# The causal mask added by DVE while it takes the maxima, and the window layers' turned keys of a batch in one row of columns

## The reference

```python
scores = jnp.einsum('bqhd,bkhd->bhqk', Q, K) / math.sqrt(D_K)
scores = jnp.where(causal, scores, -jnp.inf)
attn = jax.nn.softmax(scores, axis=-1)          # first attention
...
q = l2norm(q) * qs
k = l2norm(k) * ksc
q, k = rotary_xpos(q, k)
sim = jnp.einsum('bhwid,bhwjd->bhwij', bq, bk)  # bk: the window before, then its own
mask = (i < j) | (i > j + WINDOW) | (j == -1)
attn = jax.nn.softmax(jnp.where(mask, -big, sim), axis=-1)
```

## Time and profile before

| what | value |
|---|---|
| median of 3 runs | 1494.41 us (1487.76 to 1495.81) |
| the profiled execution | 1497.84 us |
| its span, first to last instruction | 1496.1 us |
| mean granted TensorE clock in it | 0.927 |
| busy: PE / DVE / ACT / POOL | 87% / 79% / 62% / 50% |

### The profile page before, as it was taken

How to read it: one execution, slowest core, us unless ns; L and a number is a source line. 1 busy time by engine, 2 the same in 40 slices (tenths; PEclk the granted TensorE clock), 3 DMA queues, 4 the chain that set the end, 5 groups by cost and what they waited for, 6 DMA issues and landing times. The chain is left out here.

```text
span 1496.1 us, 30910 instructions
## 1 busy us (share of the span) xinstructions
PE 1294.6 (87%) x11013; PEld 757.0 (51%) x11013; DVE 1180.9 (79%) x2532; ACT 934.8 (62%) x2597; POOL 742.3 (50%) x742
## 2 busy tenths in 40 slices
PE   5479999999999997459999999699689999997892
PEld 3234444444444443326666666565356666665551
DVE  6577888888888860659999999666599999996667
ACT  4416776777677765647888888332378888884230
POOL 2001212211221221469999999310499999993102
PEclk9859999999999997579999999889799999999896
DMA  4412121112111101100211111000002111110001
GB/s 115 132 61 68 35 60 44 37 36 60 43 37 39 33 4 50 50 21 23 51 35 31 30 30 30 8 1 1 21 23 49 30 30 30 34 32 9 1 1 56
DMA packets 35056, 55.40 MB, mean 37 GB/s; under 512 B 7106, under 2 KB 22732, under 8 KB 32588
## 3 DMA queue, kind: packets, MB, share of 16 engines
q1 hardware_dynamic: 34328, 53.27, 13.4%
q10 hardware_dynamic: 576, 0.15, 0.0%
HBM read 26.67 MB, written 8.39 MB: 23 GB/s over the span
## 5 line engine op out<-in xcount | busy, mean ns | idle before, releaser
L595 DVE TENSOR_REDUCE a_nm<-a_psM 128x1 f32<-128x512 f32 (+3 forms) x768 | 372.7, 550 | 101.8 <-PE a_psM L429 54.4
L516 ACT ACTIVATE a_prob<-a_psE 128x512 f32<-128x512 f32 (+3 forms) x768 | 319.4, 499 | 147.9 <-PE a_psE L444 146.1
L429 PE MATMUL a_psM<-a_ks,a_qs 72*128 72x512 bf16 (+3 forms) x768 | 253.0, 343 | 18.7 <-PEq L76 18.1
L444 PE MATMUL a_psE<-a_qs,a_ks 84*128 84x512 bf16 (+3 forms) x768 | 251.9, 336 | 13.2 <-ACT a_prob L516 6.9
L1080 POOL TENSOR_TENSOR w_t<-w_raw,w_sin 128x256 f32<-128x256 f32 x256 | 239.9, 966 | 47.2 <-ACT w_raw L1006 47.2
L551 POOL TENSOR_SCALAR_AFFINE_SELECT a_prob<-a_prob 128x512 f32<-128x512 f32 x128 | 81.1, 635 | 344.4 <-ACT a_prob L516 318.7
L1029 ACT ACTIVATE w_prob<-w_psS,w_bias 128x128 f32<-128x128 f32 x512 | 181.4, 367 | 49.9 <-DVE w_bias L1158 44.4
L1090 POOL TENSOR_TENSOR w_rn<-w_ssm,mhalf 128x16 f32<-128x16 f32 x64 | 189.4, 2960 | 3.1 <-DVE w_ssm L1128 3.1
L1085 POOL TENSOR_TENSOR w_rot<-w_t 128x1024 f32<-128x1024 f32 x64 | 152.0, 2374 | 8.8 <-issue 0.4
L458 PE MATMUL a_psO<-a_prob,v_all 128*32 128x512 f32 (+3 forms) x1536 | 148.1, 502 | 0.0
L444 PEld LDWEIGHTS a_psE<-a_qs,a_ks 84*128 84x128 bf16 x768 | 74.9, 98 | 142.7 <-issue 49.3
(11 more groups left out here) (139 smaller groups left out, 2508.3 us busy)
## 6 DMA issues: line engine op xcount, KB each, us to landing
w_vb<-w_v SPq DMA_DIRECT2D x128, 128.0 KB, 2.3
a_qs<-q_parts SPq DMA_DIRECT2D x16, 576.0 KB
a_ks<-k_parts SPq DMA_DIRECT2D x16, 576.0 KB
q_parts<-p_parts SPq DMA_DIRECT2D x24, 128.0 KB
k_parts<-p_parts SPq DMA_DIRECT2D x24, 128.0 KB
out_x<-l_y SPq DMA_DIRECT2D x8, 256.0 KB, 2.3
a_qs<-a_nmT SPq DMA_DIRECT2D x32, 48.0 KB
w_wqkv<-in_wqkv SPq DMA_DIRECT2D x2, 768.0 KB, 7.4
```

Source lines behind the costliest of these rows:

```text
L429: mm = pe.matmul(out, qs[0:ROWS, g, j, i * P:(i + 1) * P], ks[0:ROWS, g, j, 512 * kc:512 * kc + n], start=True, stop=not diag)
L444: pe.matmul(psE[:, r % NRING, 0:w], ks[0:KROWS, g, j, kt * P:(kt + 1) * P], qs[0:KROWS, g, j, q0:q0 + w], start=True, stop=True).then_inc( ...
L516: act.activation(prob[G % NPROB][:, j, 0:w], psE[:, r % NRING, 0:w], ACT.Exp, scale=SCALE0).then_inc(e_read, 1)
L595: dve.tensor_reduce(nm[:, s % 2, kc, i, j:j + 1], psM[:, r % MRING, 0:n], AX.X, ALU.max, negate=True).then_inc(m_read, 1)
```

## The change

In attend the mask matmul L432 goes. For the units that hold the diagonal DVE runs `tensor_tensor_reduce`: scores plus a mask of 512 columns (zeros, then the triangle), times -1, written back over the scores in PSUM, with a running minimum into the place of the negated maximum. Other units keep their reduction. In window the turned keys of the tiles of a batch lie side by side in one row of columns (two such rows, for batches in turn), so the 64 keys before a tile are already there: the copy L1151 and its semaphore go, and the score matmuls read 128 adjacent columns. The values' halves and the mask follow the new order of the keys.

```diff
--- before.py
+++ after.py
@@ -424,13 +424,9 @@
                     pe.wait_ge(stack_in[g], 32 * (s // NG + 1))
                 n = min(512, (i + 1) * P - 512 * kc)
                 out = psM[:, r % MRING, 0:n]
-                diag = kc == i // 4
                 ge(pe, m_read, r - MRING + 1)
-                mm = pe.matmul(out, qs[0:ROWS, g, j, i * P:(i + 1) * P], ks[0:ROWS, g, j, 512 * kc:512 * kc + n],
-                               start=True, stop=not diag)
-                if diag:
-                    mm = pe.matmul(out[:, n - P:n], sb["ident_b"], sb["mask_q"], start=False, stop=True)
-                mm.then_inc(m_ready, 1)
+                pe.matmul(out, qs[0:ROWS, g, j, i * P:(i + 1) * P], ks[0:ROWS, g, j, 512 * kc:512 * kc + n],
+                          start=True, stop=True).then_inc(m_ready, 1)
 
             def score(G, j):
 
@@ -585,6 +581,8 @@
         @block.vector
         def _(dve):
 
+            dve.wait_ge(sb["const_in"], 64)
+
             def maximum(u):
                 s, (i, j, kc) = u // NMU, MAX_UNITS[u % NMU]
                 r = max_slot(u)
@@ -592,7 +590,11 @@
                 if s > 1 and u % NMU in (0, NM_A):
                     dve.wait_ge(nm_parts, 2 * (s - 2) + (u % NMU == NM_A) + 1)
                 dve.wait_ge(m_ready, r + 1)
-                dve.tensor_reduce(nm[:, s % 2, kc, i, j:j + 1], psM[:, r % MRING, 0:n], AX.X, ALU.max, negate=True).then_inc(m_read, 1)
+                scores, low = psM[:, r % MRING, 0:n], nm[:, s % 2, kc, i, j:j + 1]
+                if kc == i // 4:
+                    dve.tensor_tensor_reduce(scores, scores, sb["mask_q"][:, 512 - n:512], -1.0, -3.0 * NEG, ALU.add, ALU.min, low).then_inc(m_read, 1)
+                else:
+                    dve.tensor_reduce(low, scores, AX.X, ALU.max, negate=True).then_inc(m_read, 1)
 
             def merge(s):
                 dve.wait_ge(m_read, max_slot(s * NMU + NMU - 1) + 1)
@@ -825,7 +827,7 @@
         raw = tile("w_raw", [P, 2, 2 * INNER])
         t1, t2 = tile("w_t1", [P, 2 * INNER]), tile("w_t2", [P, 2 * INNER])
         rot = tile("w_rot", [P, 2, 2 * INNER])
-        qT, kT = tile("w_qT", [P, 2, 4, P]), tile("w_kT", [P, 2, 4, KEYS])
+        qT, kT = tile("w_qT", [P, 2, 4, P]), tile("w_kT", [P, 2, 4, WIN + S])
         v = [tile(f"w_v{r}_", [P, INNER]) for r in range(4)]
         vb = [tile(f"w_vb{r}_", [P, INNER]) for r in range(4)]
         bias = tile("w_bias", [P, 2, HEADS])
...
@@ -868,8 +870,8 @@
 
                 at_least(sp, v_copied, base, t, 1)
                 halves(sp, av_done, t, -4)
-                sp.dma_start(vb[r][0:WIN, :], v[r][0:WIN, :]).then_inc(vb_in[r], 16)
-                sp.dma_start(vb[(r + 1) % 4][WIN:P, :], v[r][WIN:P, :]).then_inc(vb_in[r], 16)
+                sp.dma_start(vb[r][WIN:P, :], v[r][0:WIN, :]).then_inc(vb_in[r], 16)
+                sp.dma_start(vb[(r + 1) % 4][0:WIN, :], v[r][WIN:P, :]).then_inc(vb_in[r], 16)
 
             sp.wait_ge(zeroed, layer * 4 + 4)
             for t in range(NT):
@@ -908,21 +910,18 @@
                 p = r % 2
                 at_least(pe, qT_copied, base, t, 1)
                 at_least(pe, kT_copied, base, t, 1)
-                at_least(pe, prev_copied, base, t, 1)
                 halves(pe, exp_done, t, 0)
                 for w in range(2):
                     pe.matmul(psS[:, w, :].rearrange("p (c k) -> p c k", c=4), sb["ident_b"],
                               sb["mask_w"][:, t % TB, :].unsqueeze(1).broadcast_to((P, 4, P)), start=True, stop=False, skip_group_check=True)
+                half, first = t // TB % 2, t % TB * P
                 for c in range(4):
                     cols = slice(c * P, (c + 1) * P)
-                    for w in range(2):
-                        rows = slice(DH * w, DH * w + DH)
-                        lower = kT[rows, p, c, :].rearrange("p (a k) -> p a k", a=3)[:, 0:3:2, :]
-                        pe.matmul(psS[0:WIN, w, cols].rearrange("p (a k) -> p a k", a=2), qT[rows, p, c, 0:WIN], lower,
-                                  start=False, stop=True, skip_group_check=True)
-                    for w in range(2):
-                        rows = slice(DH * w, DH * w + DH)
-                        i = pe.matmul(psS[WIN:P, w, cols], qT[rows, p, c, WIN:P], kT[rows, p, c, 0:P], start=False, stop=True, skip_group_check=True)
+                    for u in range(2):
+                        for w in range(2):
+                            rows = slice(DH * w, DH * w + DH)
+                            i = pe.matmul(psS[WIN * u:WIN * u + WIN, w, cols], qT[rows, p, c, WIN * u:WIN * u + WIN],
+                                          kT[rows, half, c, first + WIN * u:first + WIN * u + P], start=False, stop=True, skip_group_check=True)
                 i.then_inc(s_done, 2)
 
             def turn_p(t, r, b):
@@ -1096,8 +1095,8 @@
         def _(dve):
 
             dve.memset(hT[WIN:P, 1, P:P + 1], 0.0).then_inc(zeroed, 1)
-            dve.memset(kT[:, 1, :, :], 0.0).then_inc(zeroed, 1)
-            dve.memset(vb[0][WIN:P, :], 0.0).then_inc(zeroed, 1)
+            dve.memset(kT[:, :, :, 0:WIN], 0.0).then_inc(zeroed, 1)
+            dve.memset(vb[0][0:WIN, :], 0.0).then_inc(zeroed, 1)
             dve.memset(ss[:, :, :, 1], 1e-24).then_inc(zeroed, 1)
 
             dve.wait_ge(w_in, WINDOW_LOADS)
@@ -1142,13 +1141,9 @@
                 dve.tensor_tensor(both, both, rn[:, p, :].unsqueeze(2).broadcast_to((P, 16, DH)), ALU.mult).then_inc(unit_done, 1)
 
             def copy_kT(t, r):
-                p = r % 2
                 at_least(dve, qkT_done, base, t, 1)
-                at_least(dve, prev_copied, base, t, 0)
-                dve.tensor_copy(kT[:, p, :, 0:P], psT[:, 1, :].rearrange("p (c n) -> p c n", c=4)).then_inc(kT_copied, 1)
-
-                halves(dve, s_done, t, -2)
-                dve.tensor_copy(kT[:, p, :, P:KEYS], kT[:, 1 - p, :, WIN:P]).then_inc(prev_copied, 1)
+                dve.tensor_copy(kT[:, t // TB % 2, :, WIN + t % TB * P:WIN + t % TB * P + P],
+                                psT[:, 1, :].rearrange("p (c n) -> p c n", c=4)).then_inc(kT_copied, 1)
 
             def maxima(t, r, w):
                 p = r % 2
@@ -1451,7 +1446,7 @@
             def early(name, shape, dt=F32):
                 return first.enter_context(nc.sbuf_tensor(name, shape, dt))[:]
 
-            sb["mask_q"] = early("mask_q", [P, P], BF16)
+            sb["mask_q"] = early("mask_q", [P, 512], BF16)
             sb["mask_k"] = early("mask_k", [P, P], BF16)
             sb["w_down"] = early("w_down", [P, 2 * DC])
             sb["w_uq"] = early("w_uq", [DC, D])
@@ -1496,7 +1491,7 @@
     bf, f = mybir.dt.np(BF16), np.float32
     c = {"c_ident": np.eye(P, dtype=f), "c_ident_b": np.eye(P).astype(bf)}
     i, j = np.arange(P)[:, None], np.arange(P)[None, :]
-    c["c_mask_q"] = np.where(j > i, NEG, 0.0).astype(bf)
+    c["c_mask_q"] = np.concatenate([np.zeros((P, 512 - P)), np.where(j > i, NEG, 0.0)], axis=1).astype(bf)
     c["c_mask_k"] = np.where(i > j, NEG, 0.0).astype(bf)
     sel = np.zeros((KROWS - ROWS, NG, HG, S), bf)
     for h in range(HG):
@@ -1504,10 +1499,9 @@
     c["c_sel"] = sel
 
 
-    key = np.where((j >= WIN) & (i < WIN), j - 2 * WIN, j)
-    ok = (key <= i) & (i <= key + WIN)
+    ok = (i % WIN <= j) & (j <= i % WIN + WIN)
     mask = np.broadcast_to(ok[:, None, :], (P, TB, P)).copy()
-    mask[:WIN, 0, WIN:] = False
+    mask[:WIN, 0, :WIN] = False
     c["c_mask_w"] = np.where(mask, 0.0, NEG).astype(bf)
     c["c_carry"] = np.broadcast_to((np.arange(TB) > 0).astype(f), (P, TB)).copy()
     c["c_shift"] = np.eye(P, k=1, dtype=f)
```

More of the change, by code:

```diff
@@ L846, in window @@
         v_copied, raw_done, t1_done, t2_done, rot_done, unit_done = (sem(x) for x in ("v_copied", "raw_done", "t1_done", "t2_done", "rot_done", "unit_done"))
-        qkT_done, qT_copied, kT_copied, prev_copied = sem("qkT_done"), sem("qT_copied"), sem("kT_copied"), sem("prev_copied")
+        qkT_done, qT_copied, kT_copied = sem("qkT_done"), sem("qT_copied"), sem("kT_copied")
         s_done, bias_done, exp_done = sem("s_done"), sem("bias_done"), sem("exp_done")
```

## The result

The changed kernel takes 1537.1 us (median of 4 runs, 1534.9 to 1540.6); the kernel before, with a fourth run, 1492.3. The ratio is 1.0301, 95% interval 1.0275 to 1.0326: 3% slower. The forecast was 1535 us, in a range of 1505 to 1585.

The account below looks back on a forecast made before the run. TensorE was taken to bound attention, DVE and POOL waiting on each other the window layers. Profiled 1497.8 - 10 (attention) + 51 (window) = 1538.8, less 3.4: 1535 us; forecast case 1521 to 1545, range 1505 to 1585.

Parts of the forecast that it names:

- Step 1: Window period: DVE's normalisation runs after POOL's first sine product; the second product waits 0.98 us, POOL's sum starts at 3.9.
- Step 2: Window period: without the copy, DVE's division is issued 4.5 us after POOL's first sine product, inside POOL's sum.
- Step 3: Window period: the division enters at 6.1 us, ends at 7.34; POOL's power waits 0.99 us, making the period 10.07.
- Step 4: Window period: DVE's next normalisation comes at 10.27 us, just behind POOL's new period, so the collision repeats.
- The count: Window layers: 0.93 us lost in each of 60 periods with both a division and a following power, +56 us.
- The first periods: Start of each window layer: the normalisation that falls behind POOL's sum today may not any more, -3 us.
- The tails: Window layers' tails without POOL work: -2 us off the loss.
- The accumulator's read: Attention, masked maxima: lost overlap 0.085 plus read 0.06, 0.145 us each, 4.6 us per stage; DVE 28.1 us.
- The first stage: First attention stage: DVE alone on the path, some 20 masked maxima x 0.145, +3 us.
- TensorE's return: Attention: of 1.86 us of mask matmuls per stage, 1.1 comes back; TensorE's side becomes 28.6 us.
- The rivals with DVE as the bound: Attention: DVE limits from 0.16 us per maximum; chance 0.2 with window loss (1594 at 0.28), 0.07 without collision (1500 to 1540).
- no collision: Window layers: the division still runs inside POOL's power at no cost; window -5, attention -10, 1479 us; chance 0.18.

Follow-up runs that it names:

- small copy: Changed kernel plus an unread DVE copy of 128x8 floats inside SBUF, where the old previous-key copy stood: 1477.8 us, ratio 0.9892.
- small reduction: Changed kernel plus a one-operand DVE maximum over 128x128 floats of SBUF where the old previous-key copy stood: 1535.9 us, ratio 1.0287.
- slot experiment: Changed kernel with one PSUM slot moved from the maxima (4 to 3) to the scores ACT reads (3 to 4): 1557.0 us, ratio 1.0434.
- extra ACT work: One more small ACT instruction in each attention group, added to both kernels: changed kernel 1544.0 us, kernel before 1498.3 us.

## Why the prediction was right

**Window layers: +51 us forecast with their tails (56 - 3 - 2), 50.9 measured** between first and last power of the two layers, +55 in the kernel with this part alone. The mechanism is the one forecast, step by step; that the sums agree to a tenth is in part luck, as the count below shows.
- Step 1, the normalisation colliding with the second product: as forecast. The second product starts at 798.55 and takes 1.70 us; four take 3.76.
- Step 2, the division issued 4.5 us after the first product: it is 802.42 - 797.86 = 4.56. ACT's exponentials were in time.
- Step 3, the division let in ahead of the power: forecast 7.34 us after the first product for its end, measured 805.19 - 797.86 = 7.33. The power was held 0.99 us: 3.89 less 2.90.
- Step 4, the period: forecast 10.07, measured 10.08; the normalisation was forecast 0.20 us behind the first product and comes at 808.13, 0.19 behind. The cycle holds itself.
- The count: 60 powers are held, as forecast. The last of each layer lies behind the marks, so 29 intervals per layer have the new length: 58 x 0.94 = 54.5 us.
- The first periods (-3 forecast): off the 54.5 go the irregular first periods of before, 2.6 us in layer 1 and 0.9 in layer 2. But most of the 2.6 belongs to the one profiled execution: its normalisation of 3.24 us does not come again in the kernel with the attention part alone, whose window code is that of before (longest 1.74 us), and there the layers take 283.9 and 284.5 us. Beside that kernel the changed one needs 53.0 us more between the powers (310.6 + 310.8 less 283.9 and 284.5).
- The tails (-2 forecast): not shown; the differences there are within what executions differ by.

The Trainium skill (SBUF — State Buffer, Who interferes with whom) says that a copy can contend with POOL, if it runs in a mode that takes both ports, and that a reduction never does on this chip. The small copy and the small reduction agree: the copy inside SBUF is held by POOL's sum (0.65 us instead of 0.16), the reduction is not (0.28 us). No run here shows the copy's mode. The other reading of the Trainium skill that the prediction weighed, a hold for the whole of POOL's power, is not seen: the cosines L1132 take 1.21 us inside the power after the change too.

**Attention: -10 us forecast, -9.3 to the last merge, -8 in the kernel with this part alone.** That the sum came out right is luck: the accumulator's read and the first stage were put too high, TensorE's return too. With the read at its measured price DVE needs 23.5 + 1.6 = 25.1 us per stage, far below TensorE's 28.6, and the prediction's own figure for a cheap read (0.06 us per maximum) is -18 us.
- The accumulator's read. The step "the read cannot overlap the stream" failed. The durations of the new operation and its read, by form, then some in time:

```profile
L595 DVE CUSTOM_DVE_ANT_0 a_psM<-a_psM,mask_q 128x512 f32<-128x512 f32 x128 | 86.6, 708 | 0.0
...
L595 DVE DVE_READ_ACCUMULATOR2_ANT a_nm<- 128x1 f32 x512 | 72.8, 142 | 0.0
```

```profile
310.09 0.69 DVE L595 CUSTOM_DVE_ANT_0 a_psM<-a_psM,mask_q 128x512 f32<-128x512 f32 x1
310.70 0.14 DVE L595 DVE_READ_ACCUMULATOR2_ANT a_nm<- 128x1 f32 x1
310.70 0.69 DVE L597 TENSOR_REDUCE a_nm<-a_psM 128x1 f32<-128x512 f32 x1
...
312.52 0.14 DVE L595 DVE_READ_ACCUMULATOR2_ANT a_nm<- 128x1 f32 x1
312.52 0.33 DVE L595 CUSTOM_DVE_ANT_0 a_psM<-a_psM,mask_q 128x128 f32<-128x128 f32 x1
...
312.77 0.33 DVE L595 CUSTOM_DVE_ANT_0 a_psM<-a_psM,mask_q 128x128 f32<-128x128 f32 x1
...
313.01 0.33 DVE L595 CUSTOM_DVE_ANT_0 a_psM<-a_psM,mask_q 128x128 f32<-128x128 f32 x1
```

The stream takes 708 ns where a maximum took 683, and the read is recorded with 0.14 us, but the next instruction starts at the same moment as the read (310.70; 312.52). In front of a plain maximum a masked one costs 310.70 - 310.09 = 0.61 us against 0.60; in a row of masked ones of 128 columns 312.77 - 312.52 = 0.25 against 0.20. So the price is 0.01 to 0.05 us per maximum and not 0.145 (the other widths give no more), and writing the sums back into PSUM shows no cost. Per stage 32 x 0.05 = 1.6 us at most instead of 4.6, and the kernel without any mask puts what of it reaches the end at 0.1, against 0.3 added for DVE and TensorE waiting for each other.
- The first stage. The +3 us put there for masked maxima that run ahead of all other work are not seen: the first merge starts at 108.0 us instead of 108.7, and at 106.8 to 110.4 in the other kernels with the new operation.
- TensorE's return. I took 1.1 of 1.86 us; the kernel without any mask shows 0.67. In the same 100 us the scores' waits for ACT rose from 8.7 us in 27 places to 20.0 in 70: TensorE comes to its next score earlier and finds its slot taken. That this is where the time went is read from the trace; the slot experiment shows that the waits go with a fourth slot, but not what the stage would then be, and the extra ACT work did not confirm it. The cause of the missing 0.4 us is open.

The merges were forecast 28.9 us apart and are 29.17. The rivals with DVE as the bound needed 0.16 us per maximum, three times what was measured. The rival on the other side, no collision, did not come true; the kernel with the small copy shows that it was priced well: where the division stays behind the power the program takes 1477.8 us, against the 1479 worked out for it. The range that the prediction gives beside its forecast, 1521 to 1545, does not follow from its own terms: window +56 and attention 0 make 1550.

## What to carry to other kernels

Before an instruction is taken off a full engine, look at what it waits for: one whose duration is far above its least value may be holding its successors in phase with another engine. In these traces a DVE instruction with two SBUF operands, or a DVE copy inside SBUF, and a POOL product or sum wait for each other, in the order in which they are issued; POOL's power, once it has begun, holds nothing. A long two-operand DVE instruction that is issued while one POOL instruction runs gets in ahead of POOL's next one, and POOL pays most of its length: 0.99 us of 1.22 here. A tiny copy inside SBUF in front of it gave POOL its turn, and turned a loss of 3% into a gain of 1%, about half of which is the attention part.

## What the runs showed that was not expected

- The read of DVE's accumulator is recorded with 0.14 us behind each masked maximum, but the next instruction starts with it: 0.01 to 0.05 us per operation.
- A DVE copy of eight floats per partition is held by POOL just as one of 256 is: it takes 0.16 us at the least, 2.0 at the most.
- With the small copy as a spacer the period is 9.10 us, 0.05 below the old one, since the shorter copy no longer holds POOL's power.
